# A one-core fused transformer kernel: waits for PSUM banks name the engine that empties the bank, and each such wait stands once

## What is computed

```python
x = L0_attn_x                                        # (32, 256, 128)
x = x + attn0(layernorm(x))                          # 16 heads of 8, softmax over all 256 keys
x = x + (relu(layernorm(x) @ w1 + b1) @ w2 + b2)     # width 512
x = x + attn1(layernorm(x)) @ wo.T                   # 16 heads of 8, rotary, causal
x = x + layers(layernorm(x))                         # 2 layers, see below
```

## Time and profile before

| | |
|---|---|
| runs of the kernel | 2946.74, 2946.95, 2950.72 us |
| the profiled execution, its own time | 2951.99 us |
| span of the profile | 2950.3 us |
| mean granted TensorE clock | 0.976 of full speed |
| PE busy | 2662.8 us, 90% |
| PE weight loads (PEld) busy | 1920.5 us, 65% |
| DVE busy | 2306.6 us, 78% |
| ACT busy | 2127.6 us, 72% |
| POOL busy | 1577.1 us, 53% |

### The profile page before, as it was taken

How to read it: one execution, slowest core, us unless ns; L and a number is a source line. 1 busy time by engine, 2 the same in 40 slices (tenths; PEclk the granted TensorE clock), 3 DMA queues, 4 the chain that set the end, 5 groups by cost and what they waited for, 6 DMA issues and landing times.

```text
span 2950.3 us, 68787 instructions
## 1 busy us (share of the span) xinstructions
PE 2662.8 (90%) x24276; PEld 1920.5 (65%) x24276; DVE 2306.6 (78%) x5760; ACT 2127.6 (72%) x5956; POOL 1577.1 (53%) x1749
## 2 busy tenths in 40 slices
PE   4678999999999999999999999999999999999887
PEld 2455666666666676666666666666676666666665
DVE  3457888888888888888888888888888888887763
ACT  2356787777777777777777777777777877777763
POOL 1034565565556556555655655555565555556652
PEclk7789999999999999999999999999999999999997
DMA  2000000000000000000000000000000000000000
GB/s 81 3 3 4 5 5 4 7 7 6 7 7 5 4 7 7 6 7 7 5 4 7 7 6 7 7 5 4 7 7 6 7 7 5 6 5 7 5 5 6
DMA packets 41985, 22.65 MB, mean 8 GB/s; under 512 B 21130, under 2 KB 40884, under 8 KB 41652
## 3 DMA queue, kind: packets, MB, share of 16 engines
q1 hardware_dynamic: 41652, 18.24, 2.2%
HBM read 9.86 MB, written 4.19 MB: 5 GB/s over the span
## 4 chain that ended last, share of the span: by engine, by line
PE 50%; ACT 28%; DVE 11%; POOL 4%; issue 3%; DMA 0%; POOLq 0%; SPq 0%; DVEq 0%; ACTq 0%
PE bank L1177 7%; ACT probs L756 7%; ACT P L788 6%; PE bank L1074 5%; PE bank L1257 5%; PE bank L1140 4%; DVE negmax L896 4%; PE bank L1188 4%; ACT rawP L788 3%; PE bank L1249 3%; PE bank L1118 2%; PE bank L1095 2%; PE bank L1162 2%; PE bank L1214 2%; PE bank L1208 2%
## 5 line engine op out<-in xcount | busy, mean ns | idle before, releaser
L756 ACT ACTIVATE probs<-bank 128x512 f32<-128x512 f32 (+1 forms) x1024 | 478.2, 566 | 200.5 <-PE bank L1118 199.5
L896 DVE TENSOR_REDUCE negmax<-bank 128x2 f32<-128x512 f32 (+1 forms) x896 | 549.8, 679 | 37.9 <-PE bank L1095 37.7
L1177 PE MATMUL bank<-wqkv_sb,hS 128*128 128x512 f32 x768 | 417.7, 629 | 51.1 <-ACT hS L725 28.5
L688 POOL TENSOR_TENSOR rn<-ss_kept,minus_half 128x16 f32<-128x16 f32 x128 | 373.0, 2914 | 7.5 <-DVE ss_kept L959 7.5
L633 POOL TENSOR_TENSOR veps<-moments,eps_tile 128x2 f32<-128x2 f32 x192 | 38.1, 198 | 571.6 <-DVE moments L848 571.6
L655 POOL TENSOR_SCALAR_AFFINE_SELECT probs<-probs 128x256 f32<-128x256 f32 x512 | 206.6, 427 | 218.9 <-ACT probs L756 218.8
L676 POOL TENSOR_TENSOR rawA<-rawA,rope_sb 128x512 f32<-128x512 f32 x128 | 165.1, 1289 | 281.8 <-ACT rawA L775 281.8
L1140 PE MATMUL bank<-probs,V 128*32 128x256 f32 (+1 forms) x4096 | 251.9, 364 | 17.2 <-POOL probs L655 12.0
L676 POOL TENSOR_TENSOR rawB<-rawB,rope_sb 128x512 f32<-128x512 f32 x128 | 178.9, 1398 | 113.9 <-ACT rawB L775 113.8
L945 DVE TENSOR_REDUCE ss<-P 128x8 f32<-128x512 f32 x256 | 174.4, 681 | 78.3 <-ACT P L772 78.2
L979 DVE TENSOR_REDUCE negmax<-bank 128x2 f32<-128x384 f32 (+1 forms) x384 | 206.8, 594 | 34.0 <-PE bank L1214 33.6
(11 more groups left out here) (140 smaller groups left out, 7131.9 us busy)
## 6 DMA issues: line engine op xcount, KB each, us to landing
xin<-x SPq DMA_DIRECT2D x32, 128.0 KB, 2.1
out<-xout SPq DMA_DIRECT2D x32, 128.0 KB, 1.8
feed_h<-YB SPq DMA_DIRECT2D x64, 63.5 KB
wqkv_sb<-wqkv SPq DMA_DIRECT2D x1, 1536.0 KB
feed_h<-YB SPq DMA_DIRECT2D x64, 0.2 KB
rawQ<-c_masks SPq DMA_DIRECT2D x1, 832.0 KB
w_sb<-w SPq DMA_DIRECT2D x1, 682.0 KB
w_sb<-w SPq DMA_DIRECT2D x2, 256.0 KB, 3.0
```

The source lines that it names most:

```text
L688: nc.gpsimd.tensor_tensor(rn[:, l, t].rearrange("p m h -> p (m h)"), ss_kept[:, l, t].rearrange("p m h -> p (m h)"), minus_half[:], ALU.po ...
L756: nc.scalar.activation(dst, src, ACT.Exp, scale=SCALE0 if k == ATTN0 else SCALE1)\
L896: nc.vector.reduce_max(negmax[:, k, t, head:head + 4 * many - 3:4], tile(u, e)[:, :].rearrange("p (h k) -> p h k", h=many), AX.X, negate=T ...
L1177: mm(tile(u)[:], hS[:, l, t * P:(t + 1) * P], wqkv2_sb[:, l, m * INNER:(m + 1) * INNER], start=True, stop=True).then_inc(has_filled(u), 1)
```

## The change

`places_of_evictions` works out, for every use of every bank, which engine evicts it and at which place in this engine's list. `newest` goes by these: of all evictions asked for, it keeps for each evicting engine only the one that comes last in this engine's order, and it drops those at or before a place that the waiting engine has already waited for (`reached`, emptied where an engine's program begins). Three other waits of PE now stand only at the first unit of those that shared them: `lo_ready` (Q and K of ATTN1 split), `m_ready` (the maxima in QB) and `rope_ready` (q and k rotated). No computing instruction, DMA, tile, bank or place in an order is changed; ACT's program is the same to the last wait.

```diff
+def places_of_evictions(orders, sequences):
+    place = {(engine, u.sequence, u.stream, u.number): n for engine in orders for n, u in enumerate(orders[engine])}
+    evictions = {}
+    for units in sequences:
+        for u in units.values():
+            engine = "scalar" if u.kind in ON_SCALAR or (u.kind == "qkv2" and u.part % 3 == 2) else "vector"
+            taker = u
+            if u.kind == "mix" and u.uses:
+                taker = [v for v in units.values() if v.stream == u.stream and v.kind == "mix" and v.part == u.part + GROUPS // 2][-1]
+            for n, (b, use) in enumerate(u.buffers):
+                evictions[b, use + 1] = engine, (place[engine, taker.sequence, taker.stream, taker.number], n)
+    return evictions
...
+        reached = {}
+
         def newest(*groups):
-            counts = [c for group in groups for c in group]
-            return [(emptied[c[1]], max(n for b, n in counts if b == c)) for c in dict(counts)]
+            last = {}
+            for (_, b), n in (c for group in groups for c in group):
+                engine, when = evictions.get((b, n), (b, (0, 0)))
+                if when > reached.get(engine, (-1, 0)):
+                    reached[engine] = when
+                    last[engine] = emptied[b], n
+            return list(last.values())
...
-                    else:
+                    elif u.part == 0 and u.kind == "turn_q" and u.source is None:
                         pe.wait_ge(sig("lo_ready", u), so_far("lo_ready", u))
-                    if u.source == "with maxima":
+                    if u.part == 0 and u.source == "with maxima":
                         pe.wait_ge(sig("m_ready", u), so_far("m_ready", u))
...
-                    src_done = earlier(u, "scale2", 2 if u.kind == "turn_q2" else 3)
-                    pe.wait_ge(sig("rope_ready", src_done), so_far("rope_ready", src_done) + 1)
+                    if u.part == 0:
+                        src_done = earlier(u, "scale2", 2 if u.kind == "turn_q2" else 3)
+                        pe.wait_ge(sig("rope_ready", src_done), so_far("rope_ready", src_done) + 1)
```

More of the change, by code:

```diff
@@ L308, in max_part @@
     return n // 2, 2 * (n % 2), 2
+ON_SCALAR = ("turn", "shift", "turn_q", "turn_k", "turn_q2", "turn_k2", "scores", "scores2", "up0", "turn_p",
+             "turn_max", "spread2")
 def plan():
@@ L452, in fused_block @@
         orders, sequences = plan()
+        evictions = places_of_evictions(orders, sequences)
         rises = {}
@@ L530, in run @@
             waited = rest is None
+            reached.clear()
             for u in orders[engine]:
```

## The result

The changed kernel took 2930.68 us (median of 2928.52, 2930.59, 2930.76, 2930.97) against 2947.95 for the kernel before in the same batch: ratio 0.9939, 95% interval 0.9923 to 0.9955, 17 us less. Run again in a later batch it took 2928.58 us, ratio 0.9930 (0.9917 to 0.9943). I had forecast 2941.5, 5.4 us less, with 2935 as the low end of the range. The sign was right, the size three times too small.

The account below looks back on a forecast made before the run. Time was taken to run in turn through PE and the engines emptying its banks, with only waiting time to gain. Four places gave -0.10 - 0.04 - 0.07 + 0.04 = -0.17 us, x 32 = 5.4: 2946.95 - 5.4, about 2941.5 us, range 2935 to 2947.

Parts of the forecast that it names:

- L1249: PE start after DVE's second maximum: its one separate wait goes, -0.04 us a round, between 0 and -0.06.
- Satisfied waits cost nothing while PE is ahead: On PE's queue: waits already met vanish behind the array's work, 0.02 us each at most between units of transposes.
- Rival 1: Every separate wait on PE costs: each of 3,108 gives back 0.02 us, 62 us, 2885 us; chance 0.03.
- L1149: PE start after DVE's copy: the release would pass no separate wait, 0.12 us becoming 0.05, -0.07 us a round.
- L1095: Scores behind the fillers: two separate waits become one, in ACT's seat, 0.21 us becoming 0.11, -0.10 us a round.
- L1090, +0.04 us: Masks on PE: ACT's release gets a separate wait alone, so a later start, +0.04 us a round, between 0 and +0.06.
- L1177, at nothing: PE start off the chain, released late by hS 33 times: costed at nothing because chain work goes on beside it.
- L1074, at nothing: PE transposes off the chain, released late by KB 34 times: costed at nothing because chain work goes on beside them.
- DVE and POOL, at nothing: DVE loses 448 separate waits and POOL 151: no gain counted, though one DVE place might give 2.6 us at most.
- The sum, -0.17 us x 32: Four late releases on the chain add up to -0.17 us a round; counted over 32 sequences, 5.4 us.
- Rival 2: PE runs dry so often that neighbours of the four places count too: gain 8 to 13 us, 2934 to 2939; chance 0.15.
- The bound that I worked out from the neighbours: Upper end of the gain, largest values at the four places plus two neighbours: 0.41 us a round, 13 us, 2934 us.

Follow-up runs that it names:

- extra_behind: Changed kernel with one more wait, met since the start, named behind the needed ones in each of TensorE's bank-wait lists: 2934.81 us, 0.9961 of the kernel before.
- old_mix2: Changed kernel with the old list of waits only at units mix2 and project2 of TensorE (L1270, L1278): 2934.69 us, 0.9946 of the kernel before.
- old_places: Changed kernel with TensorE's old bank waits at units maxes, mix2, project2, attn_out, turn_q and turn_k: 2945.54 us, 0.9984 of the kernel before.
- pe_only: Changed kernel with the new list of waits on TensorE alone, VectorE, GpSimd and SyncE waiting as before: 2937.00 us, 0.9960 of the kernel before.
- merge_only: Changed kernel without memory of earlier waits, still keeping only the last of several evictions by one engine: 2938.51 us, 0.9964 of the kernel before.
- after_again: The changed kernel once more with no edit, in a later batch: 2928.58 us, 0.9930 of the kernel before.

## Why the prediction was wrong

The step that failed is the walk along the chain: the sum took the late releases that matter to be four, read off the "issue" rows of one chain, priced L1249 at -0.04 us where it measured -0.13, and put everything beside the four at nothing. The mechanism held, and so did the kind of work that is free.

- *Satisfied waits cost nothing while PE is ahead*: borne out by `extra_behind`, 1.2 ns for a wait, and by the 0.17 us that stayed. Rival 1 (2885 us) is out.
- *0.05 us through an own wait, 0.11 to 0.12 through a separate one*: right, 0.06 and 0.12 at the transposes in both pairs of kernels. L1149 was forecast at -0.07 and moved by 0.06. L1095 was forecast at -0.10, and the lead grows there from 9.26 to 9.36 us; when its whole kind of unit is put back, it costs 0.17 a sequence.
- *L1249, -0.04 us*: this term failed. "The scores L1118 just before it follow probabilities from POOL, which the change does not hurry" was read off the chain, and the chain does not see a release through a separate wait: it writes "issue" and goes on to the instruction before on the same engine. What released L1249 was DVE's second maximum, and DVE came to it sooner because L914 did, because L1241 did. From L1095 on, the lead grows from 9.36 to 9.49 us at L1249: -0.13, three times my term. Half of it, 0.06, is L1241 at 1510.74, released late by an earlier maximum of DVE, through a separate wait before and its own after; my sum has it nowhere. `old_mix2` confirms it at 0.14 for the two lists together.
- *L1090, +0.04 us*: wrong sign of an effect that isn't there, the lead stays at 9.55 and 9.56. The cause is an error in what I put down ahead of the prediction. In the built program the wait for bank 3 at the masks, the own one, is that for ScalarE's eviction, and bank 6 is VectorE's; at the scores behind the fillers bank 0 is ScalarE's and bank 2 VectorE's. So ScalarE's release at the masks had the own seat before and after.
- *L1177, at nothing*: wrong, though not at the start that I priced. The one that waits for hS gains nothing: its release had the own seat already. The one at 1557.29 waits for a bank that DVE's copy `rawC` empties, through a separate wait before and through its own after. The lead grows from 9.56 to 9.60 us in this round, and by 0.06 in the median of 20 rounds. The view calls it "issue", and the chain goes past it from one PE step to the next.
- *L1074, at nothing*: right in the end. Its second unit gains 0.06 us on the first (1499.24 to 1490.05 is 9.19, 1499.92 to 1490.67 is 9.25), but the softmax scores behind it wait for ACT's qT, 0.67 us instead of 0.49, and start only 9.20 us sooner (1504.45 and 1495.25). This agrees with `old_places`.
- *DVE and POOL, at nothing*: wrong by 0.08 us a sequence (`pe_only`), 2.6 us. Some 0.06 of it is the one multiplication of DVE ahead of the masks, 1.16 against 1.10 us, whose length my sum had no term for. At L930, where I allowed 2.6 us, DVE starts 0.04 us after the reduction's end instead of 0.11, and loses it again at the next instruction.
- *The waits that were dropped as repeats*: I had no term for them; 0.19 us a sequence depend on the memory of `reached` (`merge_only`).
- *The sum, -0.17 us x 32*: the multiplication was right and the additivity too (0.35 against 0.39). Per sequence it is 0.45 to 0.48 at full clock. `old_places` accounts for 0.35 and `pe_only` for 0.08, which leaves no more than the resolution. The 0.50 to 0.52 of the raw pace holds 0.05 for the stretch at half the clock near 1190 us in the profile before, which is no gain of the change.

Rival 2 describes what came: more late places land. I gave it 0.15, since "issue" was 3% of the chain. That was the wrong measure: "issue" is the latency *not* covered by a busy engine, and the 0.06 us steps hide just as well in what a view names PE, DVE or ACT idle time. The bound that I worked out from the neighbours, 0.41 us a round, came near the truth by luck: of its two neighbours, the start at hS and the one at KB, neither gained, and the places that did gain are others. I left its far end outside the range because I trusted the chain.

## What to carry to other kernels

Where engines hand banks to each other in turn, look at which semaphore sits on the instruction itself, and give that seat to the release that comes last; the number of waits met long before matters less: 67 more of them a sequence cost 0.08 us, the seats 0.39. Cost such a change over the whole loop of hand-overs, not over the pieces of one chain: ask for each late start who released it, and take the end of that instruction from the timeline when the view says "issue". And compare kernels by the pace of a repeated instruction far from start and end, which here told 0.03 us of 85 apart where medians scattered by several us. Look up the granted clock between the two ends first, in short stretches, since a mean of 1.00 can hide 3.4 us at half.

## What the runs showed of the hardware

In these rows a release reaches a waiting weight load after 0.05 to 0.06 us when it is the instruction's own wait, and after 0.11 to 0.12 us through one instruction that only waits. On DVE it was 0.11 us through a separate wait and 0.04 after the change:

```profile
1554.17 0.29 DVE L950 TENSOR_TENSOR probs<-bank,recip 128x128 f32<-128x128 f32 x1
1554.50 0.43 DVE L958 TENSOR_TENSOR probs<-xin,probs 128x256 f32<-128x256 f32 x1
```

I had not expected that the granted clock differs from run to run of one kernel with the work unchanged, above all where PE is thinly used. In the first 75 us of the changed kernel it was 0.83 in the stretch shown above, and in `after_again`:

```profile
0.00:75.00 75.00, 35.73 (x207) 22.95 (x207) 25.61 (x86) 18.97 (x37) 13.83 (x29) 0.77 0.25 79
```

From 300 to 2580 us it was 1.00 in both. In the kernel before it fell to 0.50 for 3.4 us at 1189.5, after PE had stood idle for 0.89 us. The same idle time comes round after round without a fall, and what decides is not shown. At half the clock the transposes L1226 took 0.42 us each and at full clock 0.27:

```profile
1189.24 1.85 PE L1177 MATMUL bank<-wqkv_sb,hS 128*128 128x512 f32 x2 [0.89 <-ACT hS L725]
1190.89 0.42 PE L1226 MATMUL bank<-ident_r,rawP 128*128 128x128 f32 x1
...
1193.08 0.27 PE L1226 MATMUL bank<-ident_r,rawP 128*128 128x128 f32 x1
```
